# Scaled fp16 parts for queries, keys and row maxima, and score tiles only as wide as the causal mask needs

## What is computed

```python
xn = layernorm(x)                                   # eps 1e-5
q, k, v = heads(xn @ Wq.T), heads(xn @ Wk.T), heads(xn @ Wv.T)
scores = where(causal, -inf, q @ k.T / sqrt(32))
s = merge(softmax(scores) @ v) @ Wo.T
hidden = fwht(silu(xn @ W1.T) * (xn @ W3.T))        # 2048 wide, normalised
g = silu(hidden @ W2.T)
out = x + s * g
```

## Time and profile before

| what | value |
|---|---|
| runs | median 944.32 us of 3 (943.84 to 944.62) |
| the profiled execution | 944.66 us, its span 943.0 us |
| TensorE busy | 98% |
| VectorE busy | 77% |
| ScalarE busy | 66% |
| GpSimd busy | 36% |
| TensorE clock granted over the span | 0.999 of full |
| heads of batch 0, starts of the first and last score | 88.3 to 361.7 us |
| heads of batch 1, starts of the first and last score | 556.3 to 824.5 us |

### The profile page before, as it was taken

How to read it: one execution, slowest core, us unless ns; L and a number is a source line. 1 busy time by engine, 2 the same in 40 slices (tenths; PEclk the granted TensorE clock), 3 DMA queues, 4 the chain that set the end, 5 groups by cost and what they waited for, 6 DMA issues and landing times. The chain is left out here.

```text
span 943.0 us, 19017 instructions
## 1 busy us (share of the span) xinstructions
PE 928.3 (98%) x6500; PEld 566.6 (60%) x6500; DVE 728.0 (77%) x1416; ACT 625.5 (66%) x1340; POOL 339.0 (36%) x591
## 2 busy tenths in 40 slices
PE   8999999999999999999999999999999999999997
PEld 7764566666666656744468656566665666575443
DVE  7886998998998988846665579989898899833343
ACT  4456889989889877833344358787887888833221
POOL 1896664665665442000000114344344353410000
PEclk9999999999999999999999999999999999999999
DMA  9797245544343414661236622323323232150111
GB/s 291 270 252 228 80 114 151 143 118 118 86 121 90 118 31 124 221 226 44 67 103 244 201 57 80 91 58 95 76 75 92 61 81 58 46 202 22 45 45 45
DMA packets 57920, 110.09 MB, mean 117 GB/s; under 512 B 5600, under 2 KB 22624, under 8 KB 57312
## 3 DMA queue, kind: packets, MB, share of 16 engines
q1 hardware_dynamic: 57824, 108.88, 38.9%
HBM read 79.23 MB, written 29.36 MB: 115 GB/s over the span
## 5 line engine op out<-in xcount | busy, mean ns | idle before, releaser
L1264 DVE TENSOR_TENSOR p_lo<-stages,p_hi 128x512 f16<-128x512 f32 (+2 forms) x288 | 201.7, 710 | 25.3 <-ACT p_hi L878 23.7
L1613 PE MATMUL f<-x_hi,w_lo 128*128 128x512 f16 x512 | 195.6, 382 | 0.0
L1613 PE MATMUL f<-x_lo,w_hi 128*128 128x512 f16 x512 | 194.8, 380 | 0.0
L1613 PE MATMUL f<-x_hi,w_hi 128*128 128x512 f16 x512 | 194.5, 380 | 0.0
L868 ACT ACTIVATE stages<-s 128x512 f32<-128x512 f32 (+2 forms) x288 | 150.6, 524 | 57.9 <-PE s L1573 55.5
L878 ACT ACTIVATE p_hi<-stages 128x512 f16<-128x512 f32 (+2 forms) x288 | 160.5, 557 | 25.6 <-POOL stages L699 16.4
L1573 PE MATMUL s<-qk_st 98*128 98x512 f32 (+2 forms) x384 | 129.9, 416 | 1.7 <-DMA qk_st<-m_lo 1.5
L699 POOL TENSOR_SCALAR_AFFINE_SELECT stages<-stages 128x128 f32<-128x128 f32 x192 | 61.4, 325 | 167.9 <-ACT stages L868 167.4
L707 POOL TENSOR_TENSOR w_lo<-w,w_hi 128x256 f16<-128x256 f32 x128 | 95.5, 775 | 55.2 <-ACT w_hi L931 52.8
L1251 DVE CUSTOM_DVE_ANT_0 m<-m,causal 128x1024 f32<-128x1024 f32 (+1 forms) x98 | 104.5, 1066 | 3.8 <-PE m L1554 2.7
L986 ACT ACTIVATE h_hi<-hidden 128x1024 f16<-128x1024 f32 x32 | 33.8, 1057 | 97.1 <-PE f L1411 97.1
(11 more groups left out here) (224 smaller groups left out, 1907.9 us busy)
## 6 DMA issues: line engine op xcount, KB each, us to landing
qk_st<-qk_parts SPq DMA_DIRECT2D x96, 256.0 KB, 4.3
w<-w1w SPq DMA_DIRECT2D x32, 512.0 KB, 3.6
qk_parts<-qk_hi SPq DMA_DIRECT2D x32, 256.0 KB, 3.5
qk_parts<-qk_lo SPq DMA_DIRECT2D x32, 256.0 KB, 4.4
scan<-w1w SPq DMA_DIRECT2D x12, 512.0 KB, 5.6
wht_in<-w SPq DMA_DIRECT2D x4, 1024.0 KB, 10.6
w_butterflied<-wht_in SPq DMA_DIRECT2D x4, 1024.0 KB, 5.7
x_in<-x SPq DMA_DIRECT2D x16, 256.0 KB, 2.9
```

Source lines behind the costliest of these rows:

```text
L1264: dve.tensor_tensor(p_lo[s][:], expd[q % NE][:, 0:end - need], p_hi[s][:], ALU.subtract).then_inc(p_lo_done, 1)
L1613: mm = pe.matmul(F[m][:, 0, :], w, v, start=k == 0, stop=k == GMM - 1)
```

## The change

q and k are kept as fp16 parts. Their scales are powers of two derived from the sums of squares of wq and wk: ScalarE squares each of the eight weight tiles with an accumulated sum, TensorE sums over the partitions with a matmul of ones, and VectorE turns the sum into `qk_scale[:, m]` (m = 0 for q, 1 for k) and `qk_back`. The copies of the groups use `qk_scale` as a column operand, and the exponential uses `qk_back` as its scale. The maxima's parts are fp16 times -1/4096, against rows of 4096 instead of 1. `qk_parts` in DRAM, `qk_st`, `qk_hi`, `qk_lo`, `m_hi` and `m_lo` become fp16 (in rooms of the same bytes). Scores and the maximum of tile 0 are no longer widened. The first scale (`scale_of_qk(0)`) stands on VectorE between two halves of the statistics of the second half of x, the second after group 3; TensorE's sums stand in the first groups and after group 3.

```diff
+M_TOP = 4096.0
...
-    qk_parts = nc.dram_tensor("qk_parts", [4, D, S], F32R, kind="Internal").ap()
+    qk_parts = nc.dram_tensor("qk_parts", [4, D, S], F16, kind="Internal").ap()
...
-            qk_st = [sb(f"qk_st{i}", [P, 2, S], F32R, r) for i in (1, 2)]
+            qk_st = [sb(f"qk_st{i}", [P, 2, 2 * S], F16, r) for i in (1, 2)]
...
-            m_hi = sb("m_hi", [NT, P], F32R, r)
-            m_lo = sb("m_lo", [NT, P], F32R, r)
+            m_hi = sb("m_hi", [NT, 2 * P], F16, r)[:, 0:P]
+            m_lo = sb("m_lo", [NT, 2 * P], F16, r)[:, 0:P]
...
         def score_cols(c, k):
             need, end = max(c * W, k * P), (c + 1) * W
-            return min(need, end - 2 * P), need, end
+            return need, need, end
...
+        def wqk_sum_bank(m):
+            return (F[1], X)[m][:, 0, 0:KT]
+        def qk_scale_steps(m):
+            return (4, 9)[m]
...
             def load_weight(b, i):
                 if i >= 5:
                     sp.wait_ge(split_lo, split_no(b, i) - 4)
+                    if b == 0:
+                        sp.wait_ge(wqk_sum, i - 4)
...
+                    pool.memset(qk_ssq[:], 0.0).then_inc(ssq_ready, 1)
...
+            def wqk_squares(i):
+                act.wait_ge(ssq_ready, 3)
+                if i:
+                    act.wait_ge(wqk_sum, i)
+                act.activation(qk_squares[:], raw[i % 5], ACT.Square, accum_out=qk_ssq[:, i:i + 1]).then_inc(wqk_sum, 1)
...
-                    act.activation(qk_hi[g % NB][:], group_bank(g), ACT.Copy,
-                                   scale=SCALE if QK_GROUPS[g][1] == 0 else 1.0).then_inc(proj_hi_done, 1)
+                    m = QK_GROUPS[g][1]
+                    act.wait_ge(qk_scale_step, qk_scale_steps(m))
+                    act.activation(qk_hi[g % NB][:], group_bank(g), ACT.Copy, scale=qk_scale[:, m:m + 1]
+                                   ).then_inc(proj_hi_done, 1)
...
                     split_weight(b, KT - 1)
+                    for i in range(KT):
+                        wqk_squares(i)
...
                         for i in range(KT, 2 * KT):
                             split_weight(b, i)
+                            if b == 0:
+                                wqk_squares(i)
...
                 act.activation(expd[q % NE][:, 0:end - need], SB[q % 2][:, 0, need - start:end - start],
-                               ACT.Exp).then_inc(exp_done, 1)
+                               ACT.Exp, scale=qk_back[:, 0:1]).then_inc(exp_done, 1)
...
-                act.activation(m_hi[:], X[0:NT, 0, 0:P], ACT.Copy, scale=-1.0).then_inc(m_hi_done, 1)
+                act.activation(m_hi[:], X[0:NT, 0, 0:P], ACT.Copy, scale=-1.0 / M_TOP).then_inc(m_hi_done, 1)
...
+            def scale_of_qk(m):
+                at, done = slice(m, m + 1), 4 * m
+                power, scale = (v[:, at].bitcast(mybir.dt.int32) for v in (qk_power, qk_scale))
+                dve.wait_ge(wqk_sum_ps, m + 1)
+                dve.tensor_reduce(qk_power[:, at], wqk_sum_bank(m), axis=AX.X, op=ALU.add).then_inc(qk_scale_step, 1)
+                dve.wait_ge(qk_scale_step, done + 1)
+                dve.tensor_scalar(power, power, 1, 0x7F800000, ALU.logical_shift_right, ALU.bitwise_and
+                                  ).then_inc(qk_scale_step, 1)
+                dve.wait_ge(qk_scale_step, done + 2)
+                dve.tensor_scalar(scale, power, 0x7F800000, 0, ALU.bitwise_xor, ALU.bitwise_or
+                                  ).then_inc(qk_scale_step, 1)
+                dve.wait_ge(qk_scale_step, done + 3)
+                dve.tensor_scalar(qk_scale[:, at], qk_scale[:, at], 2.0 ** -57, 2.0 ** 60, ALU.mult, ALU.min
+                                  ).then_inc(qk_scale_step, 1)
+                if m:
+                    dve.scalar_tensor_tensor(qk_back[:], qk_power[:, 0:1], SCALE * 2.0 ** 112, qk_power[:, 1:2],
+                                             ALU.mult, ALU.mult).then_inc(qk_scale_step, 1)
...
-                    dve.scalar_tensor_tensor(qk_lo[g % NB][:], ps, SCALE if QK_GROUPS[g][1] == 0 else 1.0, hi,
+                    m = QK_GROUPS[g][1]
+                    dve.wait_ge(qk_scale_step, qk_scale_steps(m))
+                    dve.scalar_tensor_tensor(qk_lo[g % NB][:], group_bank(g), qk_scale[:, m:m + 1], qk_hi[g % NB][:],
...
-                    statistics(b, 1)
+                    statistics(b, 1, 0, 2)
+                    scale_of_qk(0)
+                    statistics(b, 1, 2, 2)
...
+                    if b == 0 and g == KT - 1:
+                        scale_of_qk(1)
...
                     products(1, 1)
+                    if b == 0:
+                        sum_of_wqk(0)
                     products(0, 2).then_inc(proj_ps, 1)
...
+                    if b == 0 and g == 3:
+                        pe.wait_ge(qk_scale_step, 1)
+                    if b == 0 and g == 6:
+                        pe.wait_ge(qk_scale_step, 5)
...
                     group(g)
+                    if b == 0 and g == KT - 1:
+                        sum_of_wqk(1)
...
+            def sum_of_wqk(m):
+                pe.wait_ge(ones_ready, 2)
+                after(pe, proj_lo_done, 3 * m)
+                pe.wait_ge(wqk_sum, (m + 1) * KT)
+                pe.matmul(wqk_sum_bank(m), ones_r[:].bitcast(F32), qk_ssq[:, m * KT:(m + 1) * KT], start=True, stop=True
+                          ).then_inc(wqk_sum_ps, 1)
...
-                bank, parts = max_parts(t) if t else (X[:, 0, 0:2 * P], [(0, 2 * P)])
+                bank, parts = max_parts(t)
```

More of the change, by code:

```diff
@@ L1090, in split_wv, with statistics @@
                                          ALU.mult, ALU.subtract).then_inc(wv_lo_done, 1)
[L1092 to L1094 removed]
+            def scale_of_qk(m):
[15 more added lines that the diff above has]
+                                             ALU.mult, ALU.mult).then_inc(qk_scale_step, 1)
+            def statistics(b, half, skip=0, count=TPC):
+                for t in range(half * TPC + skip, half * TPC + skip + count):
                     for i, (first, _) in enumerate(X_PARTS):
```

37 lines of the change are left out of this document (20 added, 17 removed).

## The result

The changed kernel takes **948.26 us** (median of 9 runs, 946.96 to 952.23) against 944.37 for the kernel before on the same chip (median of 9, one of which took 1909.61 us, a slow run that is not in the ratio): a ratio of 1.005, 95% interval 1.0037 to 1.0064. It is slower, by half a percent. The forecast was 931.0, with a chance of 0.05 for slower.

A forecast was written before the change was run, and what follows sets the result against it. TensorE's matmuls were taken as the bound; dropping 0.021 us beyond columns per fp32r matmul, plus narrower tiles, saves 0.66 us a head: 944.66 - 21.1 + 1.6 + 1.5 + 2.1 + 2.3 = 931.1, said as 931, range 926 to 939.

The forecast's parts named there:

- The narrower tiles: Two diagonal score tiles a head and tile 0's maximum, 128 columns narrower each: TensorE gains 0.16 us a head.
- I take 0.078 us for each of 12 exponentials: ScalarE's price for the exponential's scale from an SBUF column: 0.94 us a head, whatever the width.
- I charge 0.05 us a head: Step 5's score, needing step 3's exponential: margin 0.30 us used up; 1.5 us over 30 heads, bounds 0 and 0.3 a head.
- Rival C: ScalarE and VectorE pass on more: chained waits return another 0.2 us a head, start costs 4; 939.2 us, chance 0.16.
- Rival E: Slower: at step 5 the whole pointer price reaches TensorE, 0.94 us a head for 0.66 gained; 956 us, chance 0.03.
- VectorE's 1024-column maximum: First-batch heads computing w1/w3 scales: TensorE's third maximum reuses its bank without room; 0.3 us lost in seven heads, 2.1 us.
- heads 3 and 5: Heads where two large squares of w2 leave ScalarE too little idle time: 0.8 us charged each, 1.6 us.
- The start: Batch 0: ScalarE's new squares and VectorE's power-of-two chain delay TensorE by 2.3 us, bounds 1.0 and 4.0.
- Rows of maxima: DMA of the maxima in halved, 256-byte pieces: free while landing stays within 0.27 us of now.
- rival F: Slower: maxima land late; if 256-byte pieces doubled the 1.81 us, each head's first score waits 1.5 us; 979 us, chance 0.03.
- Surcharge (D): fp16 with 96 or 98 rows runs no faster on TensorE; only narrow tiles gain, 5.1 us; 942.7 us, chance 0.04.
- "all is kept" (B): The three losses in the heads vanish and the start costs 1 us: 924.6 us, chance 0.12.

The follow-up runs named there:

- e13_imm_share2: Changed kernel with all scales constant, no sums of squares at the start, and the two feed-forward matmul moves of `e12_share2`: 930.81 us.
- e15_no_scale_b1: Changed kernel with ScalarE's scaling of w1 and w3 cut from 512 to 8 columns in the second batch, pointer kept: 941.26 us.
- e1_exp_imm: Changed kernel with the exponential's scale as the constant SCALE/256 instead of a pointer to a column: 937.61 us.
- e3_before_ptr: Kernel before the change, with the exponential's scale given by pointer to a column of ones: 953.43 us, ratio 1.0102.
- e12_share2: Changed kernel with two feed-forward matmuls a head moved, from slot 1 to 2 and from slot 8 to 7: 946.71 us.
- e8_share: Changed kernel with one feed-forward matmul a head moved from slot 10 to slot 2: 945.54 us.

## Why the prediction was wrong

**What bounds the kernel, and the gain: right.** TensorE's matmuls set the heads before, and fp16 took the surcharge away. `e13_imm_share2` gives 0.66 us a head in batch 1, the very number of the forecast, `e15_no_scale_b1` 0.60. With only the exponential's scale constant it is 0.47, and the stop at the transpose holds the other 0.18. The narrower tiles' 0.16 is right for TensorE's work, but 0.06 of it went into longer stops in batch 1 and none of it is left in batch 0's sum.

**"I take 0.078 us for each of 12 exponentials": wrong row.** It was 0.094. The row compared exp with an immediate against tanh with a column, two functions; the difference of such a pair is not the price of a pointer. The Trainium skill (ScalarE: Activation LUTs, "What ACT_TABLE_LOAD costs") gives about 93 ns, and the runs agree with it (602 to 696, and 699 in the kernel before). By the prediction's own sum that moves the forecast by half a microsecond only.

**"ScalarE is late by two pointer prices since its last idle ... I charge 0.05 us a head": the step that failed.** The last idle time lies ahead of step 0's exponential, so four pointers stand in the run, not two: it grew from 4.94 to 5.22 us, 0.28 where 0.16 was counted (not four times 0.094: behind the 384-column exponential the next instruction starts only 0.02 later). TensorE's side of the race, from the same moment to step 5's score, shrank from 5.24 (694.03 to 699.27) to 5.02 (697.87 to 702.67 + 0.22, its start without the wait). That is 0.28 + 0.22 = 0.50 us against a margin of 0.30, of which some 0.05 is what even a waiting score shows between the end of its exponential and its own start (703.09 to 703.15). 0.25 us are left over, and TensorE stands for 0.28. I counted 0.31 in all, charged 0.05 a head, and so 1.5 us. The pointer costs 10.7 (`e1_exp_imm`), 9.0 with nothing else changed (`e3_before_ptr`). Even the upper bound of 0.3 us a head would have made it 9.

**"What queues behind a late exponential is its fp16 copy and VectorE's subtraction; the products with V come slots later": incomplete.** Behind the subtraction in VectorE's order stands the last maximum, and TensorE's transpose of the maxima waits for that, 0.29 us a head of batch 1. Rival C named this chain, at 0.2 us a head more than the forecast's 0.05, with a chance of 0.16; it is the mechanism that came true, at over twice its size (0.57 us a head in batch 1). Rival E put the whole pointer price (0.94 us a head) on the path and fell by its size: over 30 heads the pointer cost 0.30 us each in the kernel before and 0.36 in this one. The result is slower through several losses at once, a case that none of the rivals on that side held. The chance given to slower, 0.05, is also less than the 0.06 that E and F had by themselves.

**VectorE's 1024-column maximum, 2.1 us: right in kind, too small; heads 3 and 5, 1.6 us: right.** Maxima wait for it 4.5 us in ten places of batch 0 (0.4 before), 3.5 with the pointer away. What that costs can be read from the periods. Batch 0's plain heads (7, 9 and 11) became 0.31 us shorter, where 0.61 was forecast. Heads 3 and 5 came out 0.76 us each behind them, as charged, and heads 1, 2, 4, 6, 8 and 10 together 3.1 us, where 0.3 each, 1.8, was charged. So of the 7.3 us by which batch 0 missed, about 4.5 come from the plain heads' shortfall of 0.30, which every head has, 1.3 from this maximum and 1.1 from waits for the rows of maxima (1.5 us against 0.4 before).

**The start, 2.3 us: right for the sums, 1.1 short** for the split behind VectorE's pass over wv. The bounds of 1.0 and 4.0 held the 3.8 measured.

**Rows of maxima: right**, against rival F, which fell. From the last issue to the landing takes 1.68 us in the middle one of 32 heads, 1.77 before, so the smaller pieces land no later. In each kernel a few of the 32 take more than 2.3 us, up to 3.6 (six in the kernel before, one in the changed one, two to six in the others), and late ones make their heads wait: 1.9 us in three places here, 3.2 before. A slip in the rival, without effect: by its own numbers the gain is gone from a landing 0.7 us longer, not 0.9. Surcharge (D) and "all is kept" (B) fell too, though with both scales constant the time is 931.3, the number that was forecast for the change as written. That is a coincidence: this kernel has no sums at the start and no pointers, and the forecast had charged for both.

## What to carry to other kernels

Before an operation on a second engine is made dearer, find that engine's last idle moment ahead of the deadline and charge the price for every instance between the two, and set it, together with what the first engine gains over the same stretch, against the margin. A busy share of 66% or 1.8 us of idle time a head says nothing about it. When a scale is wanted at run time, make the product of the scales a constant and keep the pointer out of the instruction that is repeated most.

## What the runs showed that was not expected

- The price of a column operand in place of an immediate is nearly the same at 512, 384, 256 and 128 columns: 94, 91, 85 and 95 ns.
- Work moved within the stretch between an engine's last idle moment and its deadline changes nothing (`e12_share2`: 9.2 us of waits both times); moved in from outside it pays in full (`e8_share`: 3.2 us of 3.2 in batch 1).
- Lateness passes through engines that are not full (VectorE is busy 77% of the span): taking 0.85 us a head of scaling off ScalarE (two operations of 0.72 us became 0.295) removed a wait of TensorE for VectorE.
